# A scan layer and eight experts on one core: gated rows one tile earlier, three low pieces of w2 ahead of the sends, z's statistics in two steps and its scale moved

## The reference

```python
x = x + scan(ctx, layernorm(x))       # u = silu(conv(in_proj @ ctx)); delta = softplus(...)
    # state = state * exp(delta * A) + (delta * u) * B;  y = sum(state * C) + D * u
    # y * silu(z), where z = layernorm(x)
x = x + experts(layernorm(x))
    # probs = softmax(x @ Wg); the two best experts of each row; 320 slots per expert
    # h = relu(rows @ w1[e]) (256 -> 1024); expert_out = h @ w2[e] (1024 -> 256)
    # out[row] += gate * expert_out, for both experts of the row
```

## Time and profile before

| | us |
|---|---|
| median of 3 timed runs | 296.43 |
| lowest, highest | 295.77, 297.27 |
| the profiled execution's own time | 295.34 |
| its span, first to last instruction | 293.5 |
| scan stage, up to the first expert rows on TensorE | 149.7 |
| a layer of the loop, from one w2 load's issue to the next | 16.2 to 16.4 |
| from the end of the last layer's matmuls, near 282.6, to the end | 11 |

### The profile page before, as it was taken

The page is one execution under the profiler, slowest core; times in us unless marked ns, Lnnn a source line. Parts: engine busy times, 40 slices in busy tenths (PEclk is TensorE's granted clock), DMA queues, the critical chain, the costliest instruction groups (busy, mean ns, idle before and its releaser), DMA issues.

```text
span 293.5 us, 5022 instructions
## 1 busy us (share of the span) xinstructions
PE 243.5 (83%) x1564; PEld 219.7 (75%) x1564; DVE 225.5 (77%) x372; ACT 173.4 (59%) x379; POOL 213.8 (73%) x174
## 2 busy tenths in 40 slices
PE   8967693958687696896799999989999999999950
PEld 7745573647555575795789998979989898989940
DVE  3799998999999999999887569294857768494510
ACT  2799669658996774576356373654727363645200
POOL 1689599969979999998538368576676858586562
PEclk9999889799869755589999999999999999999995
DMA  7589610080006441141226752636455462635110
GB/s 165 220 247 320 228 73 0 11 315 1 0 3 212 148 142 38 38 179 39 72 81 218 222 184 71 255 131 222 177 206 176 150 230 72 241 118 178 37 53 28
DMA packets 15073, 40.38 MB, mean 138 GB/s; under 512 B 2922, under 2 KB 9900, under 8 KB 12112
## 3 DMA queue, kind: packets, MB, share of 16 engines
q1 hardware_dynamic: 11792, 33.15, 33.3%
q0 software_dynamic: 2816, 6.32, 6.3%
q10 hardware_dynamic: 448, 0.70, 0.9%
HBM read 32.72 MB, written 8.49 MB: 140 GB/s over the span
## 4 chain that ended last, share of the span: by engine, by line
POOL 21%; issue 15%; DMA 13%; PE 11%; DVE 8%; ACT 6%; POOLq 1%; DVEq 0%; ACTq 0%; SPq 0%
DMA w2raw<-in_w 10%; POOL out L491 6%; POOL w2lo L472 5%; POOL dbu L358 5%; ACT hthi L747 3%; ACT w2hi L642 3%; DVE h L1283 2%; POOL expert_rows L403 2%; DVE eo L1496 2%; DVE hc L1302 2%; PE ps L1063 2%; PE ps L1065 2%; PE ps L1064 2%; PE ps L868 1%; DMA xe<-expert_rows 1%
## 5 line engine op out<-in xcount | busy, mean ns | idle before, releaser
L358 POOL TENSOR_TENSOR dbu<-du,bsb 128x1024 f32<-128x1024 f32 x31 | 72.7, 2365 | 1.2 <-DMA bsb<-b_rows 0.9
L581 ACT ACTIVATE ps<-delta,anegs 128x255 f32<-128x255 f32 x128 | 53.1, 462 | 13.4 <-DVE h L1283 9.6
L1485 DVE SCALAR_TENSOR_TENSOR htlo<-ps,hthi 128x320 fp32r<-128x320 f32 x64 | 30.3, 486 | 34.8 <-ACT hthi L747 34.7
L846 PE MATMUL ps<-stack,sels 64*128 64x256 f32 x64 | 17.8, 366 | 31.8 <-DVE hc L1302 28.9
L868 PE MATMUL ps<-cst,hc 128*128 128x128 f32 x256 | 42.5, 320 | 1.4 <-DVE hc L1302 1.4
L472 POOL TENSOR_TENSOR w2lo<-w2raw,w2hi 128x512 fp32r<-128x512 f32 x28 | 35.6, 1297 | 10.9 <-ACT w2hi L642 10.7
L846 PEld LDWEIGHTS ps<-stack,sels 64*128 64x128 f32 x64 | 11.3, 222 | 40.2 <-issue 39.8
L1283 DVE TENSOR_TENSOR_SCAN h<-ps,dbu 128x1024 f32<-128x1024 f32 x18 | 41.1, 2281 | 0.2
L1063 PE MATMUL ps<-xthi,w1hi 128*128 (+1 forms) x124 | 39.2, 316 | 0.3 <-ACT w1hi L635 0.3
L1063 PE MATMUL ps<-hthi,w2hi 128*128 128x320 f32 x112 | 35.8, 320 | 3.6 <-POOL w2lo L472 3.6
L491 POOL DMA_INDIRECT out<-eo,dst x24 | 24.5, 1022 | 19.1 <-DVE eo L1496 13.6
(11 more groups left out here) (185 smaller groups left out, 512.7 us busy)
## 6 DMA issues: line engine op xcount, KB each, us to landing
w1raw<-in_w SPq DMA_DIRECT2D x8, 1024.0 KB
w2raw<-in_w SPq DMA_DIRECT2D x8, 1024.0 KB, 4.8
bsb<-b_rows SPq DMA_DIRECT2D x7, 1024.0 KB, 7.3
expert_rows<-fill SPq DMA_DIRECT2D x1, 2580.0 KB, 15.8
xe<-expert_rows SPq DMA_DIRECT2D x8, 258.0 KB, 5.3
out<-x SPq DMA_DIRECT2D x4, 256.0 KB, 5.2
xnat<-in_x SPq DMA_DIRECT2D x1, 768.0 KB, 7.3
xe<-expert_rows SPq DMA_DIRECT2D x8, 64.5 KB, 5.7
```

The source lines that it names most:

```text
L358: nc.gpsimd.tensor_tensor(dbu[j % DRING][:], du[:, :, None, cols(b)].to_broadcast([P, EC, 2, L]), bsb[b % 2][:, None, 2 * p:2 * p + 2, :]. ...
L581: ins = nc.scalar.activation(decays(g % SLOTS_DA)[:, c, i * L + 1:(i + 1) * L], delta[:, c, b * L + 1:(b + 1) * L], ACT.Exp, scale=anegs[: ...
```

## The change

Four things are moved, and nothing is added to the work.

- VectorE makes gated_rows(e - 1) behind hidden tile f = 3 and not 4 (layers 1 to 7).
- GpSimd sends the former layer's rows behind low piece 2 and not 1, in layers 1 to 6. In layer 7 it makes only two low pieces, and the sends stay behind the second.
- VectorE makes z's bn_stats for tiles 2 to 7 in steps 1 and 2, three tiles in each, and the aggregation in step 2 and not 3.
- GpSimd makes z's scale between softplus_d and softplus_w (p = 3) and not between softplus_delta and delta_u (p = 4).

```diff
                     if p == 3:
                         softplus_d(b + 1)
+                        if b == 0:
+                            z_rstd(2, slice(BT, TILES))
                         softplus_w(b + 1)
                     if p == 4:
                         softplus_delta(b + 1)
-                        if b == 0:
-                            z_rstd(2, slice(BT, TILES))
                         delta_u(b + 1)
...
-                for m in range(0 if e else WP // 2, WP // 2 if e == NE - 1 else WP):
+                pieces = range(0 if e else WP // 2, WP // 2 if e == NE - 1 else WP)
+                for m in pieces:
                     low_w2(e, m)
-                    if m == WP // 2 - 1 and e >= 1:
+                    if m == min(pieces[-1], WP - 2) and e >= 1:
                         send_results(e - 1)
                 fetch(e)
...
-                    if p in (1, 2, 3):
-                        ins = z_stats(range(2 * p, 2 * p + 2))
-                    if p == 3:
+                    if p in (1, 2):
+                        ins = z_stats(range(3 * p - 1, 3 * p + 2))
+                    if p == 2:
                         z_variance(range(BT, TILES), ins)
...
-                    if f == 4 and not first:
+                    if f == 3 and not first:
                         gated_rows(e - 1)
```

## The result

| | before | after |
|---|---|---|
| median of 4 runs, us | 296.48 | 288.94 |
| lowest, highest | 295.77, 297.27 | 288.53, 289.16 |
| profiled execution, its span | 295.34, 293.5 | 288.53, 286.7 |
| first expert rows on TensorE | 149.71 | 150.68 |
| layers 1 to 7, from turned results to turned results, sum of six | 98.41 | 92.45 |

The ratio is 0.9743, with an interval of 0.9716 to 0.9771: 7.6 us less, or 288.8 us on the 296.43 that stood before the forecast, 0.1 us under the low end of the range, 288.9. The forecast was 290.4, a change of 6.05 us. Sign and mechanism were as forecast, and the sizes were not: the layers gave 5.96 us where 4.1 stood, the tail 1.80 where 0.84 stood, and in this pair of profiles the scan stage became 0.97 us longer where 1.1 us less stood.

The account below looks back on a forecast made before the run. It took TensorE to bound the expert layers apart from its holes, with VectorE and GpSimd dense in the scan. Gains of 4.1 + 0.84 + 1.1, given as 6.05 us, off 296.43 made 290.4 us, range 288.9 to 293.2.

Parts of the forecast that it names:

- the layers: Expert layers 1 to 6: TensorE's waits for w2lo (3.6 us) and eo (0.5) go, 4.1 us gained, bounds 3.2 and 4.1.
- the tail: After 280 us: GpSimd's chain of sends and fetches moves forward with the earlier gated rows, 0.84 us, between 0.3 and 1.6.
- the scan stage: Up to about 149.7 us: earlier statistics and scale remove VectorE's wait for dbu, 1.1 us gained, bounds 0 and 1.25.
- The hole in TensorE: In layers 1 to 6, TensorE's idle time waiting for GpSimd's third low piece of w2: 3.6 us in six waits.
- the wait for eo: One wait of TensorE in the expert stage, 0.5 us, expected to go.
- the rule for TensorE's bound: In layers 1 to 6, every other loop falls under TensorE's own 15.66 us, so TensorE becomes the bound.
- the loop: In an expert layer, from w2raw's load through low pieces and sends to the next load: 14.4 us, 15.1 with one w1lo wait.
- rival A: Only part holds: ScalarE's decays or scan 4 take back 1.1 us, or send overlap the 0.84; 291.2 to 292.4, chance 0.21.
- Low pieces ahead of the sends: GpSimd, layers 1 to 6: low piece 2 fills the idle time before the sends, bringing the w2raw load forward by 1.27 us.
- B: Another wait replaces w2lo in the expert layers, so half of 4.1 us is kept: 292.4 to 294.9, chance 0.10.
- C: Nothing measurable: TensorE's hole moves to the fourth piece, the layer stays at 16.2 us; 294.9 to 296.4, chance 0.06.
- D: Slower: TensorE's low clock lasts past 149.7 us into layer 0; the whole layer would give 306 us, chance 0.03.

Follow-up runs that it names:

- sends-alone kernel: The kernel before with only three low pieces ahead of the sends, gated rows still behind the fifth hidden tile: 292.03 us, ratio 0.9797.
- the first experiments: Four kernels timed beside the kernel before (297.64 us) on one chip: only the scan edits 296.97, only the expert edits 291.14, changed kernel again 288.85, kernel before again 297.3.
- the two parts timed alone: The kernel before with only the two expert edits, 291.14 us, ratio 0.9759; and with only the two scan stage edits, 296.97 us, ratio 0.997.

## Why the prediction was wrong, by its steps

**The hole in TensorE, the term that was mis-sized.** The sum took 15.66 us of busy time as TensorE's own layer, and 0.57 to 0.68 us as the hole. Its own layer is 15.41. The timeline of TensorE in the kernel before, around the hole of layer 3, shows how it hid:

```profile
212.69 0.31 PE L1064 MATMUL ps<-htlo,w2hi 128*128 128x320 f32 x1
212.84 0.31 PE L1065 MATMUL ps<-hthi,w2lo 128*128 128x320 f32 x1
213.72 0.41 PE L1063 MATMUL ps<-hthi,w2hi 128*128 128x320 f32 x1 [0.57 <-POOL w2lo L472]
213.96 0.31 PE L1064 MATMUL ps<-htlo,w2hi 128*128 128x320 f32 x1
```

A product of 320 columns is drawn 0.31 us long but the next one starts 0.147 us later. At the hole, starts are 0.88 us apart, 0.73 more than that; the idle time counts only from the drawn end. The restart costs another 0.09 (0.24 to the next start). So this hole is worth 0.82 us and not 0.57. The layer could have been had from starts alone: 96 products at 0.147 and 12 turns at 0.109 us are 15.4. The six holes and the wait for eo, each measured in this way, come to 5.9 us instead of 4.1. The same error stands in the rule for TensorE's bound, 15.66, which did no harm: with both parts the loop, forecast at 14.4 to 15.1, was under 15.41 too, since no low piece comes late any more.

**The tail.** The gated rows moved by 1.0 us relative to layer 7's turned results (4.49 us behind them before, 3.50 after) and not 0.84. The tile itself is 0.88; the other 0.11 came from the earlier w2 load, for in the sends-alone kernel, where that load is early too, the distance is 4.38. The first send's 1.86 us became 1.04. The prediction had this as its best case, a gain of 1.6, and took the middle because the overlap would stay alike. The overlap did stay; what counted was where in the send the w2lo piece began. The prediction's own numbers had the piece slip back against the send by 0.44 to 0.59 us, and it slipped by 0.40, from 0.26 to 0.66; that this would free the send could not be read from the one row it had.

**The scan stage.** The rows came as worked out: statistics ready at 32.5, scan 4 at 32.53 (32.41 forecast), the scale from 34.35, softplus_w at 36.65, delta done at 41.45, no wait for dbu. The gain over many runs is 0.9 us (0.1 to 1.7; 1.1 forecast). Within this pair of profiles something like rival A took it back, by TensorE's clock and not by the two margins named there, ScalarE's decay and the later scan 4's data.

**Low pieces ahead of the sends.** The idle time did cover the third low piece. That both parts were needed was implied by adding up their steps and never worked out; each alone would do.

**The rivals and the range.** B and C did not come: no wait took the place of w2lo. D, the clock, was priced only as a catastrophe; its common form, up to 4 us in the scan stage from where the low stretches lie, had been put at 1 us, from VectorE's busy share in one profile. What that share did not show is that VectorE waits for products that stand in TensorE's queue behind others, and these take twice as long at 1.2 GHz. The size of the change also differs between the comparisons: the kernel before has a median of 297.64 on the chip of the first experiments, where the changed one has 288.85, 8.8 us apart, against 7.6 in the first comparison; the two intervals of the ratio overlap. The terms as measured, 5.96 + 1.80 + 0.9, come to 8.7, and the two parts timed alone, 7.2 + 0.9, to 8.1. The low end of 288.9 had no room for the layers' term above 4.1, which was called its top; nor does it follow from the tail's best case alone, which gives 290.4 - 0.76 = 289.6. (The sum's three terms add up to 6.04 and not 6.05, which changes nothing.)

## What to carry to other kernels

Where products overlap, measure a hole in TensorE from start to start, and TensorE's own work as count times start distance: the idle time in front of the late product is only part of what can be won, here 0.57 of 0.82 us. Compare each loop with the work of the engine that waits for it; once a loop is shorter than that, a second way to shorten it brings nothing there. Before the effect of an edit of 1 us is read from a pair of profiles, take several of each, or time the one edit alone.

## What the runs showed of the hardware

- How a send by GpSimd and a VectorE tensor_tensor of two SBUF inputs get on depends on when each begins. Layer 7's first send took 1.86 us when the w2lo piece began 0.26 us after it, and 1.04 when it began 0.66 us after. The second send in the changed kernel, 1.00 us long, met one begun 0.31 us after it and was not stretched. The last send of the kernel with the gated rows behind the third tile, begun 0.26 us into such a piece, took 1.21 us where 0.92 is usual. The Trainium skill, "SBUF — State Buffer", section "Who interferes with whom", has such an instruction contend with GpSimd's reads and not its writes. Against what the prediction said of it, this could fit the runs, if the send reads its row numbers early on; that step was not tried, and it leaves open why the stretch of 0.82 us is longer than the piece of 0.67.
- The scan stage of one and the same kernel came to its end at 149.7 and at 153.6 us. In both profiles TensorE had several stretches at 1.2 GHz before 127 us, and they lay at different places. A group of eight products, 128x256 each, took 1.88 us at 2.4 GHz and 3.60 at 1.2.
- Keeping TensorE at 2.4 GHz from 29.4 to 128.4 us took 144 products of zeros, and the kernel's median was 7 us over the one without them, 295.96 against 288.85 in another comparison.
